# Seven-product scheme in the first stage of a fused RWKV and gated-FFN kernel, with each group's k/r unit behind its quad

## What is computed

```
xn = layernorm(x)
k = xn @ Wk.T; r = xn @ Wr.T; v = r
y = wkv_scan(-exp(time_decay), time_first, k, v)     # recurrence over the 4096 tokens
attn = (sigmoid(r) * y) @ Wo.T
gate = xn @ (w_gate/127).T; up = xn @ (w_up/127).T   # 3072 hidden, integer weights
ffn  = (silu(gate) * up) @ (w_down/127).T
out  = x + attn + ffn
```

## Time and profile before

| what | value |
|---|---|
| median of 3 runs | 1299.21 us (1297.23 to 1324.13) |
| the profiled execution, its own time | 1298.55 us |
| its span (slowest core) | 1297.0 us |
| spans of all cores | 1294.2 to 1297.0 us |
| mean granted TensorE clock of the cores | 0.997 to 1.000 |
| PE, DVE, ACT busy | 99%, 70%, 39% of the span |
| first stage, from the first `gu` unit of chunk 1 to the first `out_unit` | 41.55 to 248.75 us |

### The profile page before, as it was taken

How to read it: one execution, slowest core, us unless ns; L and a number is a source line. 1 busy time by engine, 2 the same in 40 slices (tenths; PEclk the granted TensorE clock), 3 DMA queues, 4 the chain that set the end, 5 groups by cost and what they waited for, 6 DMA issues and landing times.

```text
span 1297.0 us, 18789 instructions; the slowest of 8 cores (1294.2 to 1297.0 us)
## 1 busy us (share of the span) xinstructions
PE 1280.1 (99%) x6064; PEld 586.9 (45%) x6064; DVE 913.8 (70%) x1473; ACT 511.2 (39%) x874; POOL 98.4 (8%) x190
## 2 busy tenths in 40 slices
PE   6999999999999999999999999999999999999999
PEld 4444444444444444444444444444444444444444
DVE  5666666625897777787888777688788877767721
ACT  5555455422325444432333444433242444442200
POOL 0111112000000000000000000000000000000000
PEclk9999999999999999999999999999999999999999
DMA  8566746996645445576555544568466554444121
GB/s 195 80 121 122 134 81 102 165 215 132 126 98 114 82 82 98 133 159 148 107 121 114 98 83 81 98 155 186 99 126 111 105 98 88 81 76 98 50 81 57
DMA packets 75407, 145.93 MB, mean 113 GB/s; under 512 B 31152, under 2 KB 34224, under 8 KB 75184
## 3 DMA queue, kind: packets, MB, share of 16 engines
q0 software_dynamic: 26640, 88.09, 39.1%
q1 hardware_dynamic: 23328, 50.35, 13.7%
q10 hardware_dynamic: 25344, 6.29, 3.1%
HBM read 209.72 MB, written 16.78 MB: 175 GB/s over the span
## 4 chain that ended last, share of the span: by engine, by line
PE 90%; DVE 4%; DVEq 2%; DMA 2%; issue 1%; ACT 0%; SPq 0%; ACTq 0%
PE ps L358 28%; PE ps_o L436 22%; PE ps L348 14%; PE ps L352 13%; PE ps_o L443 7%; PE ps_o L358 5%; DMA wd_bf<-x_tm 2%; DVE work L678 1%; DVEq L685 1%; DVEq L673 1%; DVE work L686 1%; DVEq L691 0%; DVE work L676 0%; DVE x_all L718 0%; DVE x_all L714 0%
## 5 line engine op out<-in xcount | busy, mean ns | idle before, releaser
L436 PE MATMUL ps_o<-wd_bf,h_act 128*128 128x512 bf16 x1536 | 342.0, 379 | 0.0
L436 PEld LDWEIGHTS ps_o<-wd_bf,h_act 128*128 128x128 bf16 x1536 | 150.3, 98 | 181.2
L348 PE MATMUL ps<-xn,ring 128*128 128x512 f16 x896 | 211.6, 379 | 2.7 <-DMA ring<-w_gu 2.5
L352 PE MATMUL ps<-xn,ring 128*128 128x512 f16 x896 | 211.7, 379 | 0.0
L549 ACT COPY work<-ps 128x512 f32<-128x512 f32 x216 | 126.3, 586 | 177.9 <-PE ps L358 172.0
L523 ACT ACTIVATE work<-work 128x512 f32<-128x512 f32 x64 | 40.3, 630 | 263.5 <-DVE work L692 263.3
L348 PEld LDWEIGHTS ps<-xn,ring 128*128 128x128 bf16 (+1 forms) x896 | 87.4, 98 | 108.0 <-issue 3.1
L352 PEld LDWEIGHTS ps<-xn,ring 128*128 128x128 bf16 (+1 forms) x896 | 87.7, 98 | 105.7
L358 PE MATMUL ps<-x_all,work 128*128 128x512 f16 x576 | 130.7, 379 | 1.5 <-ACT work L549 1.5
L443 PE MATMUL ps_o<-wo_bf,outp 128*128 128x512 bf16 x512 | 121.0, 379 | 0.0
L746 DVE TENSOR_TENSOR work<-work,ps 128x512 f32<-128x512 f32 x144 | 98.4, 684 | 16.4 <-ACT work L549 16.3
(11 more groups left out here) (79 smaller groups left out, 1266.0 us busy)
## 6 DMA issues: line engine op xcount, KB each, us to landing
ring<-w_gu POOLq DMA_DIRECT2D x72, 512.0 KB, 7.7
ring<-w_kr POOLq DMA_DIRECT2D x56, 512.0 KB, 7.4
xres<-x_tm SPq DMA_DIRECT2D x64, 256.0 KB, 4.9
out_tm<-xres SPq DMA_DIRECT2D x64, 256.0 KB, 3.0
x_all<-x_tm SPq DMA_DIRECT2D x28, 512.0 KB, 9.1
outp<-w_gu POOLq DMA_DIRECT2D x24, 512.0 KB, 7.8
wd_bf<-w_dn POOLq DMA_DIRECT2D x24, 128.0 KB, 8.6
wd_bf<-w_dn POOLq DMA_DIRECT2D x4, 768.0 KB, 24.0
```

Of the source, the lines that this page charges most:

```text
L348: ins = te.matmul(bank(kind, idx, 0), w[:, gc * D:(gc + 1) * D], xn[c % 2][:, gc, :], start=(gc == 0), stop=(gc == G - 1))
L352: ins = te.matmul(bank(kind, idx, 1), w[:, C + gc * D:C + (gc + 1) * D], xn[c % 2][:, gc, :], start=(gc == 0), stop=(gc == G - 1))
L436: te.matmul(ps_o[i % 2], h_act[c % 2][:, hg * TC + tt * D:hg * TC + (tt + 1) * D], wd_bf[:, half, hg * 512:(hg + 1) * 512], start=(hg == 0 ...
```

## The change

The first stage of after makes hidden rows 3k+3 and 3k+4 (k from 0 to 6) by quads, `quad(0, k)`, and rows 0, 1, 2 and 3s+2 by `gu` units as before. Its loop is now, for `s` in 1 to 7: `quad(0, s-1)`, `kr` unit `s` of chunk 0, and two `gu` units (row 3s+2 for chunk 0 and for chunk 1). The `kr` units of chunk 1 move out of the stage into the loop over `c`, ahead of the `out_unit`s of chunk 0. The transposes of chunk 1 go into `ps_o`, and the last of them stands between the halves of the first `kr` unit. The ring has 6 slots in this stage (two in `outp[1]`), and the quads' buffers lie in the second half of `wd_bf`, so `wd_second` waits until the quads are done.

```diff
+GU = [(0, 0), (0, 1), (0, 2), (1, 0), (1, 1), (1, 2)]
+for s0 in range(1, G):
+    GU += [(0, 3 * s0 + 2), (1, 3 * s0 + 2)]
+KR = [(c0, g0) for c0 in range(NCH) for g0 in range(G)]
...
 def acquire(kind, idx):
+    if kind == "tr" and idx >= NT:
+        te.wait_ge(sem["s_ev"], idx)
+        te.wait_ge(sem["v_ev"], idx)
+        return
+    if kind == "gu" and idx >= 6:
+        if idx % 2:
+            te.wait_ge(sem["v_cc"], CPQ * (idx // 2 - 2))
+        else:
+            te.wait_ge(sem["s_sq"], 4 * (idx // 2 - 3) + 3)
+            te.wait_ge(sem["v_hq"], 4 * (idx // 2 - 3) + 3)
+        return
...
 def quad(p, k):      # TensorE
+    if p == 0 and k == 0:
+        te.wait_ge(sem["v_h"], 4)
+    elif p == 0:
+        te.wait_ge(sem["v_zA"], k + 1)
...
     te.wait_ge(sem["v_s"], 4 * qd + 1)
+    if p == 0:
+        te.wait_ge(sem["v_h"], 5 if k == 0 else 6 + 2 * k)
     if qd >= 1:
         te.wait_ge(sem["v_cc"], CPQ * (qd - 1) + 5)
     product(bank_v[0], s1[:, 0, :], t1, True, False)
...
 # TensorE, main order
-tr(7)
-proj("kr", 0, 0, "t_k", "t_r")
+proj("kr", 0, 0, "t_k", "t_r", between=7)
 xn_ready(1)
-for s in range(1, 2 * G):
-    for i in range(3 * s, 3 * s + 3):
+for i in range(3, 6):
+    proj("gu", i, 1, "t_g", "t_u")
+for s in range(1, G):
+    quad(0, s - 1)
+    proj("kr", s, 0, "t_k", "t_r")
+    for i in range(4 + 2 * s, 6 + 2 * s):
         proj("gu", i, GU[i][0], "t_g", "t_u")
-    proj("kr", s, KR[s][0], "t_k", "t_r")
...
-        if 1 <= c < NCH - 1:
+        if c < NCH - 1:
             proj("kr", G * (c + 1) + g, c + 1, "t_k", "t_r")
         out_unit(8 * c + g)
...
 # ScalarE, in quad(p, k), behind the sixth copy
+if p == 0:
+    att_rec(k)
 # ScalarE, main order
+for s in range(1, G):
+    quad(0, s - 1)
+    att_exp(s)
+    for i in range(4 + 2 * s, 6 + 2 * s):
+        gate(i)
...
 # VectorE, in quad(p, k), behind the fourth sum
+if p == 0:
+    att_out(k)
 # VectorE, main order
+for s in range(1, G):
+    quad(0, s - 1)
+    if s + 1 < G:
+        w_sums(0, s)
+    att_max(s)
+    ffn_h(4 + 2 * s)
+    att_scan(s)
+    ffn_h(5 + 2 * s)
+    att_den(s)
```

More of the change, by code:

```diff
@@ L36 @@
 GU = [(0, 0), (0, 1), (0, 2), (1, 0), (1, 1), (1, 2)]
[L37 to L44, removed]
@@ L45 @@
-SLOT_AT = {u: q for q, u in enumerate(SLOTS)}
[L47 to L59, removed]
+for s0 in range(1, G):
+    GU += [(0, 3 * s0 + 2), (1, 3 * s0 + 2)]
+NG = len(GU)
+KR = [(c0, g0) for c0 in range(NCH) for g0 in range(G)]
@@ new lines, in quad_at, with quads_done, quad_rows @@
+def quad_at(p, k):
+    return k if p == 0 else Q0 + QP * (p - 1) + k
+def quads_done(p):
+    return Q0 + QP * p
+def quad_rows(p, k):
+    return (3 * k + 3, 3 * k + 4) if p == 0 else (2 * k, 2 * k + 1)
+SLOTS = [("tr", l0) for l0 in range(NT)] + [("gu", 0), ("gu", 1), ("gu", 2), ("kr", 0)]
+SLOTS += [("gu", 3), ("gu", 4), ("gu", 5)]
+SLOT_AT = {u: q for q, u in enumerate(SLOTS)}
+RING = [("gu", 0, 0), ("gu", 1, 0), ("gu", 2, 0), ("kr", 0, 0)]
+RING_END = [4, 5, 6, 1]
+RING_AT = {("gu", i0): GU[i0][1] for i0 in range(6)}
@@ L60, with ring_row @@
+RING_AT[("kr", 0)] = 3
+def ring_row(kind, row, c, uses, end):
+    for u in uses:
+        RING_AT[u] = len(RING)
+    RING.append((kind, row, c))
+    RING_END.append(end)
+for s0 in range(1, G):
+    for r0 in range(2):
+        ring_row("q", quad_rows(0, s0 - 1)[r0], 0, [("q", s0 - 1, r0)], PPQ * s0)
+    ring_row("kr", s0, 0, [("kr", s0)], s0 + 1)
+    ring_row("gu", 3 * s0 + 2, 0, [("gu", 4 + 2 * s0), ("gu", 5 + 2 * s0)], 6 + 2 * s0)
 NS = len(RING)
-for c0 in range(2, NCH):
+for c0 in range(1, NCH):
@@ L350, in proj @@
                     ins.then_inc(sem[done_a], 1)
+                    if between is not None:
+                        tr(between)
                     for gc in range(G):
@@ L603, in _ @@
                 ln_ev(5)
+                ln_rstd(7)
                 ln_xt(7)
+                ln_ev(6)
                 gate(2)
[L606 removed]
                 ln_ev(7)
                 att_exp(0)
[L609 to L610 removed]
+                for i in range(3, 6):
+                    gate(i)
[3 more added lines that the diff above has]
+                    for i in range(4 + 2 * s, 6 + 2 * s):
                         gate(i)
[L612 to L614 removed]
                 for c in range(NCH):
@@ L737, in w_sums, with quad @@
                     ve.tensor_sub(s4, a[:, :, 1, :], s2).then_inc(sem["v_s"], 1)
-                def quad(qd):
-                    k = qd % QP
+                def quad(p, k):
+                    qd = quad_at(p, k)
+                    rows = quad_rows(p, k)
+                    w = min(p, 1)
                     def h_tile(row, ch):
-                        return h_act[ch][:, (2 * k + row) * TC:(2 * k + row + 1) * TC]
+                        return h_act[ch][:, rows[row] * TC:(rows[row] + 1) * TC]
                     def summed(buf, src):
```

239 lines of the change are left out of this document (123 added, 116 removed).

## The result

The changed kernel takes 1349.3 us (median of four) beside 1299.0 for the kernel before on the same chip, also four; the ratio is 1.038, 95% interval 1.0325 to 1.0436. It is slower. In some executions of any of these kernels some cores run at a lower granted clock and take longer, so these are left out of the ratio, of the medians 1345.8 and 1298.9 that go with it, and of all that follows: 1566.1 of after (the other three are 1344.9, 1345.8 and 1352.8), 1324.1 of before, 1357.7 of e4, two of e5's three executions and cores 4 to 7 of the third, cores 2 and 3 of e9, four of e7's twelve and four of the seventeen of before beside it. The profiled execution took 1345.8 us with a span of 1343.9 on the slowest core, core 7; the median of the cores' spans is 1339.5, before it is 1295.1.

What follows compares the result with a forecast made beforehand. The prediction took the kernel before as bound by TensorE's number of matmuls. It summed 1298.6 - 12.1 (matmuls) - 3.8 (opening) + 40 (waits) + 6 (clock) + 1 (chunk 0 loop) = 1329.7, given as 1330, range 1314 to 1345.

Steps and rivals of the forecast that it cites:

- the loop of chunk 0: Loop behind the first stage, taking over eight recurrences: put at 1 us, 8 if a flip and landing wait add up.
- Matmuls removed: First stage: seven quads of 56 replace 28 gu units of 16, 56 matmuls fewer at 0.2158, 12.1 us off.
- The opening: Before the first stage: the 3.76 us wait ahead of a transpose goes, 3.8 us off, or 2 if table loads cost more.
- The ring: First-stage group: chain of waits through VectorE and ScalarE, 28.5 us against 22.44 of TensorE work, about 6.0 lost per group.
- The 40 us of waits: First stage: six seams between quads 36.4 us, the first quad about 1.5, the stage's end 2; together 40 us.
- The clock: Six gaps between first-stage quads: slower matmuls behind each cost 1.0 us a gap, 6 us; bounds 0 and about 2.5.
- My own sign of being wrong: Loop of chunk 0: out_units more than 10.4 us apart would show the prediction wrong; two other signs were also named.
- the first: Rival for the first stage: same chain of waits without a loss of clock, 1323.7 us; chance 0.22.
- the second: Rival for the first stage: TensorE stays the bound, only seven bank waits of 0.4 us, 1285.5 us; chance 0.09.
- the third: Rival: six gaps at 2.5 us of clock loss, 1339, or 1346 with 8 us for late chunk 0 landings; chance 0.15.
- The fourth: Rival for the first stage: the scheme brings no matmuls less, 1342 us; chance 0.02 together with the rest.

Runs made afterwards that it cites:

- e4: Changed kernel with w_o's second half loaded in four pieces during the first stage and w_down's second halves issued one ring load earlier: 1337.8 us.
- e5: Changed kernel with ln_flip (the DMA that transposes a token tile) issued behind att_exp in every loop over c: cores 0 to 3 spanned 1331.0 to 1339.7 us.
- e9: The same kernel as e5, run again because four cores of that one were disturbed: 1340.1 us.
- e7: Changed kernel with all four edits, those of e2, e3, e4 and e9: 1294.7 us, ratio 0.9974 to the kernel before.
- e1: Changed kernel with 72 small matmuls into an idle bank ahead of the opening wait of quads 1 to 6 of the first stage: 1340.7 us.
- e2: Changed kernel with att_rec and att_out moved out of the first stage's quad, behind it and behind att_max: 1312.6 us.
- e3: Changed kernel with the next quad's four weight sums moved behind att_max on VectorE: 1323.4 us.
- e8: Changed kernel with the edits of e4 and e9 together, the first stage left as it was: 1336.4 us.
- e6: Changed kernel with the edits of e2 and e3 together: 1306.0 us.

## Why the prediction was right, and where it was wrong

The direction and most of the size were right: 1330 foretold, with 1314 to 1345 as range; the profiled execution took 1345.8, the median of four is 1349.3. The range didn't hold it. One step failed, the loop of chunk 0: it was put at 1 us and measured 15.3 with what it does to the seam behind it.

- *Matmuls removed*: 6008, each at 0.2158, 12.1 us. Right.
- *The opening*: 3.8 foretold, 2.1 measured on core 7. The wait for `ffn_h` ahead of the transposes is gone, as said. On this core a gap of 2.3 us was followed by 16 matmuls that took 2.41 and 3.10 in place of 1.89 each, so 1.7 went there. The 3.76 us came from core 3, before's slowest; before's other cores waited 0 to 2.0 at that transpose. Their first unit of the stage starts at 38.7 to 40.2 before and at 37.6 to 39.4 after, so by the cores' medians the opening gained only 1 us.
- *The ring*: 28.5 us foretold; 28.76 measured in e1 at full clock. The 40 us of waits are 208.2 - 167.5 = 40.7 in e1. That the edits of e2 and e3 shorten it by 4.5 and 2.6, and together bring it to 22.83, shows the links. Right, with one misreading: I put the wait ahead of the third product, for `h_act`. It stands ahead of the first, for `zA` (L729), and only 1.1 us is left for the third. The quad's opening wait is for `zA` of the group's own recurrence; I had taken that to be long past. The sum wasn't touched by it, since both waits hang on one chain.
- *The clock*: 6 foretold, in the stage 5.0 (213.3 - 208.2). Right for the six gaps, at 0.8 a gap net, and in part by luck: per gap the 8 matmuls take 1.3 to 1.7 us more, more than the 1.0 I took, but part of that lies in the third product's wait, which I had held impossible ("so it isn't hidden"). I had no term for the clock behind the waits of the chunk 0 loop and its seam, and it is 6.3 us on core 7. A part of that too replaces waits: on core 3 the seam's matmuls took their 1.89 and TensorE then waited 1.39 us for a copy. The Trainium skill, "TensorE: Matmul & The Clock Gate", section on HAM oscillation, has it that an engine that runs dry in every tile is slowed in every tile: the rows at 77.81, 106.68 and 225.19 agree, and all six seams of core 7 do; the 1.68 us gaps of e3, with 8 matmuls at 1.89 behind each, show that not every gap does it.
- *The loop of chunk 0*: this is the step that failed. "I cost this at 1; if a flip and a landing wait add up, 8", and "Behind that loop nothing changes". Measured were 9.6 in the loop and 5.7 behind it, 15.3 in all, where I had 1: all but 2 us of the profiled execution's miss. By the rows of core 7, waits make 8.7 of it (3.17, 2.50 and 3.07) and the slow matmuls behind them 6.3. My own sign of being wrong, `out_unit`s more than 10.4 us apart, came true: 92.5 / 8 = 11.6 on the mean. I had the row of the flip that held ScalarE for 10.8 us (that row, like the landings, is core 3's and not core 5's), and set it against the slack of a `kr` unit on TensorE. I didn't ask what stands behind the flip in ScalarE's queue: before, no recurrence at all in this loop, and TensorE ran through although core 4's issue took 14.8; after, the Exps of a recurrence, and behind those VectorE's scans, `xres` and the input sums of chunk 2. And I let a delay end where TensorE's wait ends, while VectorE carried it on to the next seam. e8 shows that with the flip's issue short and behind the Exps the same loop runs without a wait; e4 alone gives nearly as much by median span and leaves a wait of 5.27 us on one core, e9 alone leaves 1.2 to 4.4 us in the loop.
- *The rivals*: the first (no loss of clock) fell by the six slow groups of matmuls; the second (TensorE stays the bound) is what e6's stage became, and not after's; the third, with 8 us for late landings, names the right place, but its 1346 lies near the measured time by luck: it has 15 us for the clock in the six gaps, where 5 were, and 8 for the loop, where 15.3 were. The fourth fell by the count of matmuls.

The sum as it should have been: 1298.6 - 12.1 - 2.1 + 40.7 + 5 + 15.3 = 1345.4, against 1345.8 measured. Its terms are read from the result, so that they add up tests nothing.

Why the DMA issue takes that long stays open. In the stretch from 252 to 313 us the DMA engines of core 7 are busy 95% of the time, and moving the second halves ahead cut the longest issue from 11.9 to 15.6 us in after to 6.3 or less in e4 and e8. But on core 1 of e8 the engines are busy 95% of the same stretch too (1.02 from 278 to 290), with no issue over 2.2 us, and in e7 the flip is held for 11.6 us or more with the second halves moved ahead. A version without that transfer wasn't tried, nor one with the `kr` unit away from its quad.

## What to carry to other kernels

When work is regrouped, walk once around the group through the queues of all engines and add durations with every table change: if the sum is over the bound engine's work for one group, the difference is paid every time, whatever the busy shares say. Where a stretch takes over work, look for long issues on each queue and ask what now stands behind them; and follow a delay on a non-bound engine until it has slack, since the bound engine may pay it much later. Functions that need the same activation table belong side by side: here moving two functions for that gave back 31 of the 44 us by median span, 4 of them through the clock.

## What the runs showed of the hardware

- The issue of one `DMA_TRANSPOSE` on ScalarE's queue took 1.2 us usually, 10.8 on core 3 and 14.8 on core 4 before, 15.6 on core 7 after and 19.7 on core 2 in e6, and the ACTIVATEs behind it waited. Every long one fell where the DMA engines were nearly full (shares of 1.0 and more while it lasted), but full engines don't make it long by themselves: on core 1 of e8 the share is 1.02 from 278 to 290, and the two issues in it took 2.1 and 1.3 us.
- A gap of 4.2 to 4.3 us on TensorE made the next 8 matmuls take 3.21 to 3.57 us in place of 1.89; one of 1.68 us did nothing. In between both happened: behind 2.30 us on core 7 of after they were slow, behind 3.27 on its core 3 (428.02) and 3.76 on core 3 of before they weren't. Small matmuls in the six gaps (e1) brought the stage's granted clock back to 1.00, and that was worth 5 us, not the sum of what the slow rows show, since a wait behind them hid the rest.
